# One scan of 1024 columns per state, with block 1's first value put in by a one-column product

## The chip, the cores and the metric

The kernel runs on one core of one Trainium2 chip. The metric is device time in microseconds from the start to the end of one launch. The five engines of the core each work through their own queue of instructions in program order and wait for one another by semaphores: TensorE (PE in the views, its weight loads PEld), VectorE (DVE), ScalarE (ACT), GpSimd (POOL) and SyncE (SP), which issues the DMAs.

## What is computed

Four layers follow one another on an input of 2 rows x 2048 tokens x 128 channels: a time-mix layer, a ternary feed-forward layer, a selective state-space layer and a mixture of experts. The change lies in the third:

```python
def _L1_attn_ref(x, W_in, conv_w, conv_b, W_x, W_dt, b_dt, A_log, D, W_out):
    ...                                   # raw, gate <- x @ W_in; h = silu(conv(raw) + conv_b)
    ts, Bmat, C = jnp.split(h @ W_x, [DTR, DTR + DST], axis=-1)
    dt = softplus(ts @ W_dt + b_dt)
    A = -exp(A_log)
    dA = exp(dt[..., None] * A)
    dBu = dt[..., None] * Bmat[:, :, None, :] * h[..., None]
    state = dA * state + dBu              # over the 2048 tokens, for 256 channels x 16 states
    y = sum over the states of state * C
    y = (y + h * D) * silu(gate)
    return y @ W_out
```

## The kernel before

The state-space layer (`phase_ssm`) keeps channels on partitions: 256 channels are two blocks (CB = 2) of 128 partitions, and tokens are the columns. The 2048 tokens of a row are cut in four pieces (t = 0 to 3) of N = 512 columns, and the pieces of the two rows (b = 0, 1) take turns, so that there are eight tiles (t, b). Within a tile the 16 states (n = 0 to 15) come one after the other. For each state:

- TensorE spreads row n of B over all partitions into a bank of PSUM with one bf16 product ("the spread product", line 1517, target `bcastB(n)`, which is the second block's half of `DD`; `DD` has two such pairs of banks, taken in turn, so that the product for state n waits until the scan of state n - 2 is done).
- ScalarE makes `dA` = exp(dt * -A), one instruction of 512 columns per block (line 1643).
- VectorE multiplies `dtu` (dt * h, both blocks) by the spread row, over both banks in one instruction of 1024 columns (line 1794, called dBu here), and then scans each block by itself: two instructions of 512 columns (line 1781), each starting from that block's column of `carry`.
- GpSimd multiplies the scanned states by the spread row of C (line 1734) and keeps the last column in `carry` (line 1727).
- TensorE adds the product to the sum over states with identity products in f32 (line 1503, three states later).

In between stand pieces of the next tile's preparation and of the last tile's end. On TensorE, after the spread product of state n: centring (n = 0, line 1421), variance (n = 1, 1426), the convolution in four parts (n = 2 to 5, line 1432), the gate's projection (n = 6, 1439), the skip product (n = 7), the x-projections (n = 8, 9, line 1446), dt (n = 10, 1453), and the last tile's output (n = 12 and 14). VectorE normalises the next tile after the scan of state 1 (line 1764, `xn`), for which the convolution waits, and scales the last tile's output after state 15 (line 1771). GpSimd adds and multiplies `dt` and `dtu` of the next tile at n = 12 and 13 (lines 1703, 1707). All of this order is written out by hand; no scheduler moves anything.

In the listings below, the scan and the product dBu of VectorE stand as one row each; a name like `pD` is the tile `DD`, `const` the identity, and `sel` the selectors of the spread product.

Of the kernel before, what the change touches and what calls it, by code (L numbers as in the profile page):

```python
# [5 lines left out]
F32 = mybir.dt.float32  # L6
# [28 lines left out]
for _name, _count in (  # L35
# [10 lines left out]
         "dt dtu bcastB c_out c_in0 c_in1 c_in2 c_in3 warm dA dBu scan kept prod acc y ygated skips "  # L46
# [1251 lines left out]
def phase_ssm(nc, G):  # L1298
# [9 lines left out]
    with mem:  # L1308
# [24 lines left out]
        carry = sb("carry3", [P, B, DST, CB])  # L1333
        raw = sb("raw3", [P, 2, 2 * FFN])
        YB = [mem.enter_context(nc.psum_tensor(f"pY3_{c}", [P, N], F32)) for c in range(CB)]

        DD = mem.enter_context(nc.psum_tensor("pD3", [P, 2 * CB, N], F32))
        c_rows = nc.dram_tensor("ssm_c", (NT * B, DST, N), F32, kind="Internal").ap()
# [20 lines left out]
        def dBu(n, c):  # L1359
            return DD[:, (n % 2) * CB + c, :]  # L1360

# [19 lines left out]
        def _(sp):  # L1381
# [8 lines left out]
            def rows_out(t, b):  # L1390
                sp.wait_ge(S["whole"], at(t, b))
                sp.dma_start(c_rows[t * B + b, :, :], rest[3 * BC - DST:3 * BC, b, :]).then_inc(S["c_out"], 16)

# [7 lines left out]
            rows_out(0, 0)  # L1401
            for t in range(NT):
                for b in range(B):
                    for n in range(DST):
# [7 lines left out]
                        if n == 12 and not (t == NT - 1 and b == B - 1):  # L1412
                            rows_out(*after(t, b))

        @block.tensor
        def _(pe):
# [94 lines left out]
            def body(t, b):  # L1511
                for n in range(DST):
# [4 lines left out]
                    nc.tensor.matmul(bcastB(n), G.sel[:, n, :], split[:, b, :], start=True, stop=True)\  # L1517
# [35 lines left out]
        def _(act):  # L1553
# [131 lines left out]
            act.wait_ge(S["carry0"], 3)  # L1685
# [5 lines left out]
        def _(pool):  # L1691
            def prep(t, b, step):
# [12 lines left out]
                elif step == 3:  # L1705
                    pool.wait_ge(S["dt"], at(t, b))
                    nc.gpsimd.tensor_tensor(dtu[:, b, :, :], dt[:, b, :, :], h[b][:, :, :], ALU.mult)\
                      .then_inc(S["dtu"], 1)

# [48 lines left out]
        def _(dve):  # L1758
# [15 lines left out]
            def scan(t, b, n):  # L1774
# [5 lines left out]
                for c in range(CB):  # L1780
                    last = nc.vector.tensor_tensor_scan(hs[:, slot(b, n), c, :], dA[:, slot(b, n), c, :],  # L1781
                                                        dBu(n, c), carry[:, b, n, c:c + 1],
                                                        ALU.mult, ALU.add)
                last.then_inc(S["scan"], 1)

            def body(t, b):
                for n in range(DST):
                    if n == 0:
                        dve.wait_ge(S["dtu"], at(t, b))
# [4 lines left out]
                    nc.vector.tensor_tensor(DD[:, (n % 2) * CB:(n % 2) * CB + CB, :], dtu[:, b, :, :],  # L1794
# [819 lines left out]
```

## Time and profile before

| what | us |
|---|---|
| median of 3 runs | 1310.34 |
| lowest and highest run | 1308.96, 1311.38 |
| span of the profiled execution | 1360.4 |
| scan stage in it, first dBu to last scan | about 485 |
| VectorE busy in the span | 986.3 (72%) |
| TensorE busy in the span | 1107.5 (81%) |

The profiled execution spans 1360.4 us, 50 us more than the median of the runs shown; durations below are from the profiled one. The views group instructions by line (with mean time of one), or list them in order of time, with the idle time of the engine before an instruction and the instruction that ended it. In the list of an engine, an instruction with a count (x4) is that many in a row, and its time is from the first start to the last end. PE's matmuls in f32 stand as two records each.

### The profile page before, as it was taken

To read this page: it belongs to the slowest core of one execution; us is meant where nothing else is said; L and a number is where in the kernel's file an instruction comes from. 1 tells how busy PE (TensorE), PEld (TensorE's weight loads), DVE (VectorE), ACT (ScalarE), POOL (GpSimd) and SP (SyncE) were. 2 spreads that over 40 slices of the span, in tenths; PEclk is the share of its full clock that TensorE was granted. 3 is DMA by queue.
4 is the path that set the end of the run, shared out by engine and by line. 5 is a ranking of instruction groups with operands and counts; after the bars stand their busy time and mean duration, and the time that the engine had idled before them with its cause. 6 is when DMAs were issued, how large, how long until landed. Compare 5 with 4: busy or idle time off the path is not lost. (4 is left out here: it accounts for less than half of the span.)

```text
span 1360.4 us, 16588 instructions
## 1 busy us (share of the span) xinstructions
PE 1107.5 (81%) x4914; PEld 554.2 (41%) x4914; DVE 986.3 (72%) x1333; ACT 730.8 (54%) x1163; POOL 733.0 (54%) x617
## 2 busy tenths in 40 slices
PE   6564779999999988797988989897883877877863
PEld 2221234444444423243333334332342665666653
DVE  6996775675755449999999999999928644544545
ACT  5765544555555366675766767575533333333444
POOL 0122342331413007898898898979831665656554
PEclk8775899999999988999999999998885989889886
DMA  6000000000000022332323222222101111111115
GB/s 218 0 1 0 0 1 1 0 1 0 0 0 1 0 63 80 90 98 68 107 64 102 88 83 70 76 72 68 57 8 54 37 42 38 42 39 44 36 37 185
DMA packets 32552, 67.07 MB, mean 49 GB/s; under 512 B 5760, under 2 KB 5952, under 8 KB 32256
## 3 DMA queue, kind: packets, MB, share of 16 engines
q1 hardware_dynamic: 27056, 55.16, 12.7%
q0 software_dynamic: 4992, 10.23, 2.9%
q8 instruction: 39, 0.64, 0.2%
q10 hardware_dynamic: 432, 0.76, 0.2%
q14 instruction: 33, 0.27, 0.1%
HBM read 56.57 MB, written 9.57 MB: 49 GB/s over the span
## 5 line engine op out<-in xcount | busy, mean ns | idle before, releaser
L1734 POOL TENSOR_TENSOR prod<-hs,csb 128x1024 f32<-128x1024 f32 x128 | 301.9, 2358 | 142.3 <-DVE hs L1781 141.6
L1781 DVE TENSOR_TENSOR_SCAN hs<-dA,carry,pD 128x512 f32<-128x512 f32 x256 | 313.8, 1267 | 5.6 <-DVE pD L1794 1.2
L1503 PE MATMUL pY<-prod,const 128*128 128x512 f32 x512 | 244.6, 601 | 1.8 <-POOL prod L1734 1.8
L1643 ACT ACTIVATE dA<-dt,negA 128x512 f32<-128x512 f32 x256 | 168.0, 713 | 17.2 <-POOL dt L1703 15.7
L1794 DVE TENSOR_TENSOR pD<-dtu,pD 128x1024 f32<-128x1024 f32 x128 | 155.7, 1216 | 9.2 <-PE pD L1517 9.1
L2507 DVE SCALAR_TENSOR_TENSOR hid<-pR,silu 128x512 f32<-128x512 f32 x78 | 53.8, 689 | 133.0 <-ACT silu L2215 114.6
L1503 PEld LDWEIGHTS pY<-prod,const 128*128 128x128 f32 x512 | 96.7, 192 | 117.7 <-issue 112.7
L2215 ACT ACTIVATE silu<-pR 128x512 f32<-128x512 f32 x78 | 46.5, 596 | 137.0 <-remote 77.2
L2280 POOL DMA_INDIRECT moe_outs<-y,to x78 | 84.0, 1077 | 66.3 <-ACT y L2207 45.6
L2261 POOL DMA_INDIRECT g<-moe_rows,source x78 | 79.6, 1020 | 68.5 <-issue 35.0
L1998 PE MATMUL pR<-x,moe_hi 128*128 128x256 f16 x312 | 92.3, 296 | 14.7 <-DVE x L2491 6.9
L987 ACT ACTIVATE stage<-pR,vec 128x512 f32<-128x512 f32 x64 | 43.9, 688 | 100.1 <-PE pR L687 99.9
L2000 PE MATMUL pR<-x,moe_lo 128*128 128x256 f16 x312 | 91.7, 294 | 5.5 <-issue 5.3
L1999 PE MATMUL pR<-x,moe_hi 128*128 128x256 f16 x312 | 91.8, 294 | 2.3 <-issue 1.9
L1432 PE MATMUL pQ<-xn,convw 128*128 128x512 f32 x112 | 61.6, 676 | 17.4 <-DVE xn L1764 17.4
L2110 PE MATMUL pY<-moe_hi,hid_hi 128*128 x312 | 64.1, 235 | 7.9 <-issue 7.2
L2111 PE MATMUL pY<-moe_lo,hid_hi 128*128 x312 | 63.7, 235 | 4.2 <-issue 4.2
L1037 POOL TENSOR_TENSOR z_lo<-z,z_hi 128x512 f16<-128x512 f32 x8 | 10.6, 1326 | 104.9 <-DVE z_hi L1124 104.9
L429 POOL TENSOR_TENSOR o<-o,rs 128x512 f32<-128x512 f32 x8 | 12.2, 1528 | 101.9 <-DVE o L549 101.9
L2112 PE MATMUL pY<-moe_hi,hid_lo 128*128 x312 | 63.8, 235 | 2.6 <-issue 2.6
L1517 PE MATMUL pD<-split,sel 96*128 96x512 bf16 x128 | 50.0, 391 | 19.0 <-DVE hs L1781 18.4
L1026 POOL TENSOR_TENSOR K_lo<-kstage,K_hi 128x512 f16<-128x512 f32 x24 | 28.8, 1205 | 53.7 <-DVE K_hi L1099 53.7
(422 smaller groups left out, 2591.0 us busy)
## 6 DMA issues: line engine op xcount, KB each, us to landing
csb<-ssm_c SPq DMA_DIRECT2D x128, 256.0 KB, 3.2
raw<-moe_w SPq DMA_DIRECT2D x12, 512.0 KB, 4.9
room<-moe_outs SPq DMA_DIRECT2D x8, 512.0 KB, 7.6
hidw<-hid_w SPq DMA_DIRECT2D x1, 2048.0 KB, 10.1
moe_rows<-xt SPq DMA_DIRECT2D x8, 256.0 KB, 2.0
outT<-X SPq DMA_DIRECT2D x8, 256.0 KB, 2.0
X<-xT SPq DMA_DIRECT2D x3, 512.0 KB, 4.2
g<-moe_rows,source POOLq DMA_INDIRECT x78
```

The costliest lines, as they stand in the source:

```text
L1503: last = nc.tensor.matmul(YB[c][:], G.ident, prod[:, slot(b, n), c, :], start=n == 0, stop=n == DST - 1)
L1643: last = nc.scalar.activation(dA[:, slot(b, n), c, :], dt[:, b, c, :], ACT.Exp, scale=negA[:, c, n:n + 1])
L1734: nc.gpsimd.tensor_tensor(prod[:, slot(b, n), :, :], hs[:, slot(b, n), :, :], csb[:, slot(b, n), :, :].to_broadcast([P, CB, N]), ALU.mult)\
L1781: last = nc.vector.tensor_tensor_scan(hs[:, slot(b, n), c, :], dA[:, slot(b, n), c, :], dBu(n, c), carry[:, b, n, c:c + 1], ALU.mult, ALU.add)
L1794: nc.vector.tensor_tensor(DD[:, (n % 2) * CB:(n % 2) * CB + CB, :], dtu[:, b, :, :], bcastB(n).unsqueeze(1).to_broadcast([P, CB, N]), ALU. ...
L1998: nc.tensor.matmul(out, w_hi, x_hi, start=start, stop=False)
L1999: nc.tensor.matmul(out, w_hi, x_lo, start=False, stop=False)
L2000: return nc.tensor.matmul(out, w_lo, x_hi, start=False, stop=stop)
L2110: nc.tensor.matmul(out, hid_hi[:, n % HR, at], w_hi, start=u == 0 and h == 0 and r == 0, stop=False)
L2112: last = nc.tensor.matmul(out, hid_lo[:, n % HR, at], w_hi, start=False, stop=u == 1 and h == 1 and r == 1)
L2261: nc.gpsimd.indirect_dma_start(g[:, i % GR, r, :], None, rows, bass.IndirectOffsetOnAxis(ap=source[:, 2 * i + r:2 * i + r + 1], axis=0))\
L2280: nc.gpsimd.indirect_dma_start(outs, bass.IndirectOffsetOnAxis(ap=to[:, 2 * i + r:2 * i + r + 1], axis=0), y[:, i % YR, r, :], None).then_ ...
```

## The change

The two scans of a state become one of 1024 columns that runs through both blocks. For this the first column is made to carry the start values. `dA`'s first column is fixed for good: 1 for block 0, 0 for block 1, so ScalarE's instructions now make 511 columns. `first` holds, per tile, block and state, the value of the first token: decay times carry plus fresh input. Block 0 gets it as the scan's initial value, with dBu's first column at 0 (column 0 of `dtu` is set to 0 for block 0). Block 1 gets it through dBu's first column: `dtu`'s first column is set to 1 there, and a new product of TensorE, the identity times one column of `first` in f32, overwrites column 0 of the spread row.

`first` is made once per tile: ScalarE computes the first token's decay (two instructions, 16 columns each), GpSimd does three small products and sums and two one-column fills after `dtu`, and SyncE sends the first column of B to memory and back, spread over the partitions (two more DMAs per tile). VectorE's wait for `dtu` at a tile's start becomes a wait for `first`, and TensorE waits for `first` at state 0 too. For the very first tile VectorE makes `first` itself.

```diff
+            def first_B(t, b):
+                sp.wait_ge(S["b_out"], 16 * at(t, b))
+                wait_past(sp, S["first"], at(t, b) - B)
+                sp.dma_start(B0[:, b, :], b_first[t * B + b:t * B + b + 1, :].to_broadcast([P, DST])).then_inc(S["b_in"], 16)
...
-                    nc.tensor.matmul(bcastB(n), G.sel[:, n, :], split[:, b, :], start=True, stop=True)\
+                    nc.tensor.matmul(bcastB(n), G.sel[:, n, :], split[:, b, :], start=True, stop=True)
+                    if n == 0:
+                        pe.wait_ge(S["first"], at(t, b))
+                    nc.tensor.matmul(bcastB(n)[:, 0:1], G.ident, first[:, b, CB - 1, n:n + 1], start=True, stop=True)\
                       .then_inc(S["bcastB"], 1)
...
-                    last = nc.scalar.activation(dA[:, slot(b, n), c, :], dt[:, b, c, :], ACT.Exp,
+                    last = nc.scalar.activation(dA[:, slot(b, n), c, 1:N], dt[:, b, c, 1:N], ACT.Exp,
...
+            def decay_first(t, b):
+                act.wait_ge(S["dt"], at(t, b))
+                wait_past(act, S["carried0"], at(t, b) - 2)
+                for c in range(CB):
+                    last = nc.scalar.activation(decay0[:, c, :], negA[:, c, :], ACT.Exp, scale=dt[:, b, c, 0:1])
+                last.then_inc(S["decay0"], 1)
...
+                    if not is_last(t, b) and n == 14:
+                        decay_first(*after(t, b))
...
+                    first_token(t, b)
+
+            def first_token(t, b):
+                pool.wait_ge(S["decay0"], at(t, b) - 1)
...
+                nc.gpsimd.tensor_tensor(first[:, b, :, :], decay0[:, :, :], carry[:, b, :, :].rearrange("p n c -> p c n"),
+                                        ALU.mult).then_inc(S["carried0"], 1)
+                pool.wait_ge(S["b_in"], 16 * at(t, b))
+                pool.wait_ge(S["dtu"], at(t, b))
+                nc.gpsimd.tensor_tensor(fresh0[:, :, :], dtu[:, b, :, 0:1].to_broadcast([P, CB, DST]),
+                                        B0[:, b, :].unsqueeze(1).to_broadcast([P, CB, DST]), ALU.mult).then_inc(S["fresh0"], 1)
+                pool.wait_ge(S["carried0"], at(t, b) - 1)
+                pool.wait_ge(S["fresh0"], at(t, b))
+                nc.gpsimd.tensor_tensor(first[:, b, :, :], first[:, b, :, :], fresh0[:, :, :], ALU.add)
+                nc.gpsimd.memset(dtu[:, b, 0, 0:1], 0.0)
+                nc.gpsimd.memset(dtu[:, b, 1, 0:1], 1.0).then_inc(S["first"], 1)
...
-                for c in range(CB):
-                    last = nc.vector.tensor_tensor_scan(hs[:, slot(b, n), c, :], dA[:, slot(b, n), c, :],
-                                                        dBu(n, c), carry[:, b, n, c:c + 1],
-                                                        ALU.mult, ALU.add)
-                last.then_inc(S["scan"], 1)
+                nc.vector.tensor_tensor_scan(hs[:, slot(b, n), :, :].rearrange("p c n -> p (c n)"),
+                                             dA[:, slot(b, n), :, :].rearrange("p c n -> p (c n)"),
+                                             both_dBu(n).rearrange("p c n -> p (c n)"), first[:, b, 0, n:n + 1],
+                                             ALU.mult, ALU.add).then_inc(S["scan"], 1)
...
-                        dve.wait_ge(S["dtu"], at(t, b))
+                        dve.wait_ge(S["first"], at(t, b))
```

In TensorE's order, state 6 of a tile of the middle loop stood like this before (the spread product, the gate's projection, the sum over states):

```order
L1517 MATMUL pD<-split,sel 128x512 [waits ssm_scan]
L1438 REGISTER_ALU
L1439 MATMUL pQ_0<-xn_1,ssmw 128x512 [waits ssm_parked]
L1438 REGISTER_ALU
L1439 MATMUL pQ_1<-xn_1,ssmw 128x512 [waits ssm_parked]
L1503 MATMUL pY_0<-prod,const 128x512 [waits ssm_prod]
L1503 MATMUL pY_1<-prod,const 128x512
```

and stands like this with the change:

```order
L1534 MATMUL pD<-split,sel 128x512 [waits ssm_scan]
L1537 MATMUL pD<-first,const 128x1
L1455 REGISTER_ALU
L1456 MATMUL pQ_0<-xn_1,ssmw 128x512 [waits ssm_parked]
L1455 REGISTER_ALU
L1456 MATMUL pQ_1<-xn_1,ssmw 128x512 [waits ssm_parked]
L1520 MATMUL pY_0<-prod,const 128x512 [waits ssm_prod]
L1520 MATMUL pY_1<-prod,const 128x512
```

One f32 product of one column has come in behind each spread product; nothing else moved. At a tile's start TensorE had, before, the spread product of state 0, the sum of the last tile's state 13, and the centring of the next tile:

```order
L1295 ISA [waits ssm_split3]
L1517 MATMUL pD<-split,sel 128x512 [waits ssm_scan]
L1499 ISA
L1503 MATMUL pY_0<-prod,const 128x512 [waits ssm_prod]
L1503 MATMUL pY_1<-prod,const 128x512
L1295 ISA
L1295 REGISTER_ALU [waits ssm_relu]
L1421 ISA [waits ssm_scaledC]
L1421 MATMUL pQ_0<-X,const 128x512
```

and has now:

```order
L1295 ISA [waits ssm_split3]
L1534 MATMUL pD<-split,sel 128x512 [waits ssm_scan]
L1537 MATMUL pD<-first,const 128x1 [waits ssm_first]
L1516 ISA
L1520 MATMUL pY_0<-prod,const 128x512 [waits ssm_prod]
L1520 MATMUL pY_1<-prod,const 128x512
L1295 ISA
L1295 REGISTER_ALU [waits ssm_relu]
L1438 ISA [waits ssm_scaledC]
L1438 MATMUL pQ_0<-X,const 128x512
```

The sum of state 13 and all that follows now stand behind the wait for `first`. On GpSimd, states 12 to 14 of a tile stood like this before (`dt`, then `dtu` of the next tile):

```order
L1703 TENSOR_TENSOR dt<-dt,dtu 128x1024 [waits ssm_log1p]
L1734 TENSOR_TENSOR prod<-hs,csb 128x1024 [waits ssm_acc,ssm_c_in1,ssm_scan]
L1727 COPY carry<-hs 128x2
L1707 TENSOR_TENSOR dtu<-dt,h 128x1024 [waits ssm_dt]
L1734 TENSOR_TENSOR prod<-hs,csb 128x1024 [waits ssm_acc,ssm_c_in2,ssm_scan]
```

and stand like this now:

```order
L1732 TENSOR_TENSOR dt<-dt,dtu 128x1024 [waits ssm_log1p]
L1782 TENSOR_TENSOR prod<-hs,csb 128x1024 [waits ssm_acc,ssm_c_in1,ssm_scan]
L1775 COPY carry<-hs 128x2
L1736 TENSOR_TENSOR dtu<-dt,h 128x1024 [waits ssm_dt]
L1746 TENSOR_TENSOR first<-decay_3,carry 128x32 [waits ssm_kept,ssm_decay0]
L1750 TENSOR_TENSOR fresh_3<-dtu,B_3 128x32 [waits ssm_dtu,ssm_b_in]
L1754 TENSOR_TENSOR first<-first,fresh_3 128x32 [waits ssm_fresh0,ssm_carried0]
L1755 MEMSET dtu 128x1
L1756 MEMSET dtu 128x1
L1782 TENSOR_TENSOR prod<-hs,csb 128x1024 [waits ssm_acc,ssm_c_in2,ssm_scan]
```

Five small instructions have come in between `dtu` and the product of state 14.

## Rows read from the trace of the kernel before

**Rows 1.** Groups by line, scan stage 505.5 to 995 us: count, busy us and mean ns, idle before.

```profile
L1781 DVE TENSOR_TENSOR_SCAN hs<-dA,carry,pD 128x512 f32<-128x512 f32 x256 | 313.8, 1267 | 5.6 <-DVE pD L1794 1.2
...
L1794 DVE TENSOR_TENSOR pD<-dtu,pD 128x1024 f32<-128x1024 f32 x128 | 155.7, 1216 | 9.2 <-PE pD L1517 9.1
...
L1727 POOL COPY carry<-hs 128x2 f32<-128x2 f32 x128 | 24.1, 188 | 0.0
```

**Rows 2.** VectorE in order of time, one tile: start us, us, engine, line [idle before].

```profile
763.58 1.23 DVE L1794 TENSOR_TENSOR pD<-dtu,pD 128x1024 f32<-128x1024 f32 x1 [0.41 <-PE pD L1517]
764.85 2.45 DVE L1781 TENSOR_TENSOR_SCAN hs<-dA,carry,pD 128x512 f32<-128x512 f32 x2
767.23 1.23 DVE L1794 TENSOR_TENSOR pD<-dtu,pD 128x1024 f32<-128x1024 f32 x1
...
789.88 1.23 DVE L1794 TENSOR_TENSOR pD<-dtu,pD 128x1024 f32<-128x1024 f32 x1 [0.33 <-PE pD L1517]
...
797.12 1.21 DVE L1794 TENSOR_TENSOR pD<-dtu,pD 128x1024 f32<-128x1024 f32 x1
```

**Rows 3.** TensorE in order of time, the same tile, states 2 to 5.

```profile
756.00 2.77 PE L1432 MATMUL pQ<-xn,convw 128*128 128x512 f32 x4 [2.48 <-DVE xn L1764]
...
763.16 0.38 PE L1517 MATMUL pD<-split,sel 96*128 96x512 bf16 x1
763.38 1.88 PE L1432 MATMUL pQ<-xn,convw 128*128 128x512 f32 x4
765.10 1.88 PE L1503 MATMUL pY<-prod,const 128*128 128x512 f32 x4
766.82 0.38 PE L1517 MATMUL pD<-split,sel 96*128 96x512 bf16 x1
```

**Rows 4.** TensorE's f32 products of 8 columns elsewhere: their weight loads; granted clock (PEclk) there.

```profile
1020.78 0.97 PEld L2018 LDWEIGHTS pX<-gatew,sgate 128*128 128x128 f32 x8
1020.80:1021.80 1.00, 1.00 (x12) 0.95 (x9) 0.32 (x1) 1.00 (x3) 0.92 (x1) 1.00 0.66 256
```

**Rows 5.** Groups by line and shape, whole span: shorter scans of VectorE.

```profile
L2379 DVE TENSOR_TENSOR_SCAN so_far<-keep,chosen 128x256 f16<-128x256 f16 x1 | 0.7, 691 | 0.0
L2392 DVE TENSOR_TENSOR_SCAN tiles_to<-one,tiles_of 128x8 f32<-128x8 f32 x1 | 0.2, 174 | 0.0
```

**Rows 6.** Order of time at a tile's start: GpSimd, VectorE and TensorE.

```profile
743.49 2.37 POOL L1707 TENSOR_TENSOR dtu<-dt,h 128x1024 f32<-128x1024 f32 x1
...
747.42 1.22 DVE L1794 TENSOR_TENSOR pD<-dtu,pD 128x1024 f32<-128x1024 f32 x1
...
743.37 0.39 PE L1517 MATMUL pD<-split,sel 96*128 96x512 bf16 x1 [1.50 <-DVE hs L1781]
...
747.67 1.12 PE L1421 MATMUL pQ<-X,const 128*128 x2 [2.19 <-DVE scaled L1771]
```

**Rows 7.** Busy time by stretch (PE, PEld, DVE, ACT, POOL), then granted clock: convolution of two tiles.

```profile
757.10:760.40 3.30, 3.30 (x6) 1.24 (x5) 3.29 (x3) 2.40 (x4) 1.38 (x3) 0.50 0.36 72
...
817.00:820.40 3.40, 3.40 (x9) 1.42 (x8) 3.37 (x4) 3.40 (x6) 1.50 (x3) 1.00 0.32 100
```

**Rows 8.** VectorE in order of time: the last step of a tile (three of seven).

```profile
624.79 0.67 DVE L1771 TENSOR_TENSOR scaled<-pQ,sq 128x512 f32<-128x512 f32 x1
...
807.96 0.66 DVE L1771 TENSOR_TENSOR scaled<-pQ,sq 128x512 f32<-128x512 f32 x1
...
927.83 0.67 DVE L1771 TENSOR_TENSOR scaled<-pQ,sq 128x512 f32<-128x512 f32 x1
```

**Rows 9.** One small instruction of GpSimd elsewhere: ns of it (shortest, median, longest).

```profile
L2250 POOL IOTA spare<- x1: 184/184/184, 1007.6 to 1007.6; 128x78 int32 x1
```

**Rows 10.** Start of the stage: the first DMA of C's rows, VectorE's dtu; landing times of eight.

```profile
499.59 0.33 SPq L1392 DMA_DIRECT2D ssm_c<-sq  x1
...
504.62 1.23 DVE L1836 TENSOR_TENSOR dtu<-dt,h 128x1024 f32<-128x1024 f32 x1
...
DMA to landing us min/median/max: 1.6/2.9/3.2
```

More of the change, by code:

```diff
@@ L45 @@
          "h xproj ts_in split1 whole rest1 split2 split3 dt_in magnitude expm log1p relu "
-         "dt dtu bcastB c_out c_in0 c_in1 c_in2 c_in3 warm dA dBu scan kept prod acc y ygated skips "
+         "dt dtu b_out b_in decay0 carried0 fresh0 first spliced bcastB c_out c_in0 c_in1 c_in2 c_in3 warm dA dBu scan kept prod acc y ygated skips "
          "down squaredC varianceC logC rstdC scaledC addedC w_in0 w_in1 w_high w_scaled w_low "
@@ L1333, in phase_ssm @@
         carry = sb("carry3", [P, B, DST, CB])
+        decay0 = sb("decay0_3", [P, CB, DST])
+        fresh0 = sb("fresh0_3", [P, CB, DST])
+        first = sb("first3", [P, B, CB, DST])
+        B0 = sb("B0_3", [P, B, DST])
         raw = sb("raw3", [P, 2, 2 * FFN])
@@ L1337, in phase_ssm @@
         DD = mem.enter_context(nc.psum_tensor("pD3", [P, 2 * CB, N], F32))
+        b_first = nc.dram_tensor("ssm_b", (NT * B, DST), F32, kind="Internal").ap()
         c_rows = nc.dram_tensor("ssm_c", (NT * B, DST, N), F32, kind="Internal").ap()
@@ L1401, in _ @@
             rows_out(0, 0)
+            first_B(0, 0)
             for t in range(NT):
@@ L1413, in _ @@
                             rows_out(*after(t, b))
+                        if n == 13 and not (t == NT - 1 and b == B - 1):
+                            first_B(*after(t, b))
         @block.tensor
@@ L1708, in prep @@
                       .then_inc(S["dtu"], 1)
+                    first_token(t, b)
+            def first_token(t, b):
+                pool.wait_ge(S["decay0"], at(t, b) - 1)
+                if is_start(t):
+                    pool.wait_ge(S["carry0"], 4)
+                else:
+                    pool.wait_ge(S["kept"], state(t, b, 0) - 1 - DST * (B - 1))
+                nc.gpsimd.tensor_tensor(first[:, b, :, :], decay0[:, :, :], carry[:, b, :, :].rearrange("p n c -> p c n"),
[9 more added lines that the diff above has]
+                nc.gpsimd.memset(dtu[:, b, 1, 0:1], 1.0).then_inc(S["first"], 1)
             def tail(t, b, step):
@@ L1793, in body @@
                     wait_past(dve, S["scan"], state(t, b, n) - 2)
-                    nc.vector.tensor_tensor(DD[:, (n % 2) * CB:(n % 2) * CB + CB, :], dtu[:, b, :, :],
+                    nc.vector.tensor_tensor(both_dBu(n), dtu[:, b, :, :],
                                             bcastB(n).unsqueeze(1).to_broadcast([P, CB, N]), ALU.mult)\
@@ L1836, in _ @@
             nc.vector.tensor_tensor(dtu[:, 0, :, :], dt[:, 0, :, :], h[0][:, :, :], ALU.mult).then_inc(S["dtu"], 1)
+            dve.wait_ge(S["b_in"], 16)
+            dve.wait_ge(S["dtu"], 1)
+            nc.vector.tensor_tensor(first[:, 0, :, :], dtu[:, 0, :, 0:1].to_broadcast([P, CB, DST]),
+                                    B0[:, 0, :].unsqueeze(1).to_broadcast([P, CB, DST]), ALU.mult).then_inc(S["fresh0"], 1)
+            dve.wait_ge(S["fresh0"], 1)
+            nc.vector.memset(dtu[:, 0, 0, 0:1], 0.0)
+            nc.vector.memset(dtu[:, 0, 1, 0:1], 1.0).then_inc(S["first"], 1)
             tiles(dve, body)
```

9 lines of the change are left out of this document (7 added, 2 removed).

## The prediction

> **What bounds the kernel now.** I read the groups by line of the scan stage first, then VectorE's and TensorE's instructions in order of time, then the granted clock by stretch. By the groups VectorE looks like the bound: 313.8 us of scans and 155.7 us of dBu, with 9.1 us lost to TensorE [rows 1], in a stage of about 485 us. The list in order of time says more. Left alone, VectorE needs 3.62 us per state (789.88 to 797.12 is two states) [rows 2]. From 763.58 to 789.88 it goes at TensorE's pace: at 763.58 it has stood 0.41 us for the spread product, and it starts the next dBu 3.65 us later [rows 2]. TensorE is full there: from one spread product to the next is 0.22 for itself, 1.72 for a part of the next tile's preparation and 1.72 for the sum over states, 3.66 us, with no gap [rows 3]. The seven states up to 789.88 took 26.30 us, 3.76 each, since the last two hold dearer products. So about half of a tile is TensorE's and the other half VectorE's; the two differ by hundredths of a microsecond per state, and the idle time charged to TensorE (9.1 us) is small only because both run nearly level.
>
> A tile has three legs, which I use for the sum. Leg A, from the convolution's start (756.00) to dBu of state 11 (789.88): 33.88 us, TensorE's. Leg B, from there to the next tile's first dBu: to 807.96 is 18.08, and 0.58 for the step that stands there makes 18.66, VectorE's. Leg C, from the first dBu (747.42) to the convolution: 8.58, VectorE's, since the convolution waits for xn. Together 61.12 [rows 2, 3, 6, 8]. Five tiles from 624.79 to 927.83 average 60.61 [rows 8].
>
> **What the change removes.** One scan instruction per state. A scan of 512 columns takes 1.267 us, the pair 2.45 from first start to last end [rows 1, 2]. One of 1024 adds 512 columns to the first: at 2.085 ns a column (between 8 and 256 columns) it takes 2.334 and saves 0.12; at 2.25 (between 256 and 512) 2.42, which saves 0.03 [rows 1, 5]. I take 0.12: the 256-column scan is f16, and the pitch of two f32 scans in a pair (2.45 - 1.27 = 1.18) leaves just 0.12 over 512 columns at 2.085. The ends stay for the range. If VectorE were the bound everywhere, 128 x 0.12 = 15 us would be the gain.
>
> "VectorE: DVE Perf Modes" of the Trainium skill, section on the TRN2 errata, has a fixed term of about 150 cycles per instruction, 156 ns; by it the same sum would be 20 us, while the pair's own pitch here leaves 0.12 us [rows 1, 2].
>
> **What it adds on TensorE.** A one-column f32 product per state, two records with a weight load each. No such product is in the trace; the nearest are the f32 products of 8 columns, whose 8 loads take 0.97 us at full clock, 0.12 per record, back to back [rows 4]. One load more can lie under the spread product, but the sum's first load, which lay there before, now comes out: two loads are added, 0.25 us per state. Lower end 0, if all lies under streaming products; upper end 0.37, three loads' worth, if none is covered. I take 0.25, the row nearest in kind.
>
> Leg A: at full clock it would be 32.1 before, for of its first 7.58 us (to 763.58) about 1.8 are the half clock seen from 757.10 to 760.40 (0.50, the 1.2 GHz level) [rows 2, 3, 7]. Nine new products (states 3 to 11) add 2.25: **34.35**. VectorE alone would now need 9 x 3.50, so TensorE holds it from state 6 or so.
>
> Leg B: five states at 0.12 less, 18.66 - 0.60 = 18.06, if `first` is there in time. `dtu` ends at 745.80, 1.62 before the first dBu (747.42) [rows 6]; with VectorE 0.36 faster over the three states in which GpSimd works on it, 1.26 are left. Between come three GpSimd instructions of 32 columns and two fills; small ones take 0.18 to 0.19 whatever they do [rows 1, 9], so five are 0.9 and the waits of one on the other 0 to 0.15 each: 0.9 to 1.3. Then the one-column product, 0.25 and its way to VectorE, 0.2 (the spread product needed 0.42 from start to dBu [rows 2, 3]). I take 1.5 in all and so a stall of 0.25 per tile (0.1 to 0.6): **18.31**.
>
> Leg C: VectorE's own is 8.58 - 2 x 0.12 = 8.34. But TensorE now stands still for `first`: it had been free from 741.87 and had done the sum of state 13 at 743.6; all that now starts at about 747 [rows 6]. From `first` on it must do the new product (0.25), the sum (1.72), the centring (0.86), spread and new product (0.47), sum (1.72), variance (0.86), again 0.47 and 1.72: 8.1 us, 7.6 after the first dBu. That fits in 8.34 at 2.4 GHz. But TensorE has then stood some 4.5 us with one spread product in it. Before, a wait of 2.48 us stood just ahead of the half clock at 757 [rows 3, 7], and the waits of 1.50 and 2.19 at the tile's start [rows 6] did not slow what followed. I expect the half clock at the tile's start instead of at the convolution, for about the 3.3 us it lasted before, of which 2.7 fall on work: 1.35 us lost, leg C **8.97**; and none at the convolution, since TensorE then reaches it about when xn does.
>
> Steady tile: 34.35 + 18.31 + 8.97 = 61.6 against 60.6: +1.0, six times +6. The first tile: +2.25 in leg A, -0.6 - 0.24 and +0.25 elsewhere, and at its start +0.8 (VectorE's own small steps and the product in front of the first dBu): +2.5. The new DMAs there are hidden: the first goes out with C's at 499.59, two landings of 1.6 to 3.2 end by 506.3 at the latest, about when dtu ends (505.85) [rows 10]. The last tile has fewer products beside the states, so VectorE's: at most -16 x 0.12 = -1.9, I take -1. Sum +7.5 us; the profiled span is 1360.4, 3.8% above the median, and scaling 7.5 by that changes nothing. **1310.3 + 7.5 = 1318.**
>
> **Costed at nothing.** ScalarE's 511 columns instead of 512; its two small decays, which wait for `dt` as its next instruction did anyway. Behind them now stands the output's last root; `dt` is ready before 743.49 and VectorE wants the root about 3.3 us later [rows 6, 8], room for four activations. SyncE's two DMAs per tile stand in a queue that runs four states ahead of GpSimd (`csb` has four slots); the second follows a weight transfer at n = 13 and has those four states to land. GpSimd's product of state 14 comes 1 us later; TensorE's sum of it comes later still.
>
> **Rivals.** (a) *The loads are hidden*, and VectorE's gain comes through. Leg A is then 32.1, B 18.2, C about 8.5: 58.8, 1.8 less per tile, with the first and last tiles -13 us: **1298**, faster. It decides at a product price under about 0.12. For it: loads run beside streaming products all through [rows 3, 7]. Against it: with 8 columns there is no stream to hide under, and the loads set the pace [rows 4]. "TensorE: Matmul & The Clock Gate" (step by step, the load phase) of the Trainium skill has loads pulled ahead of running matmuls, and (back-to-back issue gap) a floor of about 25 ns for so short a matmul; here a record took five times that [rows 4]. (b) *Half the price*, 0.12: 33.2 + 18.3 + 8.7 = 60.2, with the ends of the stage about **1308 to 1312**, no change. (c) *Two half-clock stretches per tile*, one at `first` and one at the convolution as before: 1.8 more per tile, **1328**. For it: the wait for xn is still there if VectorE is held longer than I think. (d) *The scan saves nothing* (1024 columns cost two of 512): legs B and C lose 0.84 per tile, **1324**.
>
> **How the numbers follow.** Forecast (1313 to 1322) 0.48; (a) 0.19; (b) 0.15, mostly within 0.2%; (c) 0.14; (d) 0.04. A measurement tells about 0.2%, 2.6 us, from no change. Faster 0.20, same 0.14, slower 0.66. The range 1302 to 1328 leaves out about half of (a) and the far end of (c).
>
> **What would show it.** In the changed trace: one scan of about 2.33 us per state; in states 6 to 11 dBu at a pitch of 3.90 us, with idle before it put down to the one-column product; TensorE without gaps there; at the tile's start a wait of over 4 us on TensorE for `first`, the clock at 0.50 behind it, and 1.00 at the convolution. A pitch of 3.66 in states 6 to 11 would show the price of the product wrong; a wait of VectorE for `first` of over 0.6 us, GpSimd's five instructions; a half clock at the convolution, the leg C.

## The result, and the profile after

The changed kernel is slower: 1338.8 us (median of four runs, 1336.1 to 1339.4) against 1309.7 for the kernel before in the same session, a ratio of 1.0201 with a 95% interval of 1.0178 to 1.0224. The forecast had the sign right and the size wrong: +7.5 us were expected and about +28 came (26 by the ratio, 29 by the medians), 11 us above the upper end of the range.

The groups of the whole run, from the page of the changed kernel (line, engine, operation, count; busy us, mean ns; idle time before it and what ended it):

```profile
L1828 DVE TENSOR_TENSOR_SCAN hs<-dA,first,pD 128x1024 f32<-128x1024 f32 x128 | 300.4, 2347 | 5.2 <-DVE pD L1841 0.8
L1841 DVE TENSOR_TENSOR pD<-dtu,pD 128x1024 f32<-128x1024 f32 x128 | 156.0, 1218 | 32.3 <-PE pD L1537 31.8
...
L1537 PE MATMUL pD<-first,const 128*128 128x1 f32 x256 | 37.9, 217 | 23.5 <-POOL dtu L1756 22.1
```

Against [rows 1]: the scans went from 313.8 to 300.4 us busy, one of 2.347 us in place of a pair, as the change means. VectorE's wait for TensorE ahead of dBu rose from 9.1 to 31.8 us. The scan did its part, then, and TensorE took it back with more. A group that was too small for the first page is as telling, VectorE's copy of three columns (the convolution's overlap with the last tile): count, shortest, median and longest ns, first and last start, of the kernel after and of the kernel before:

```profile
L1810 DVE COPY xn<-xn x6: 2006/2007/2243, 579.4 to 903.3; 128x3 f32<-128x3 f32 x6
```

```profile
L1762 DVE COPY xn<-xn x6: 141/144/145, 573.4 to 874.9; 128x3 f32<-128x3 f32 x6
```

The same instruction on the same 128x3 elements, untouched by the diff, takes fourteen times as long.

**Where in the tile.** VectorE of the changed kernel in order of time: dBu of the states 6, 9 and 11 (680.85), the tile's end (698.40), and on to the next normalized input:

```profile
660.98 1.23 DVE L1841 TENSOR_TENSOR pD<-dtu,pD 128x1024 f32<-128x1024 f32 x1
...
672.58 1.23 DVE L1841 TENSOR_TENSOR pD<-dtu,pD 128x1024 f32<-128x1024 f32 x1 [0.24 <-PE pD L1537]
...
680.85 1.23 DVE L1841 TENSOR_TENSOR pD<-dtu,pD 128x1024 f32<-128x1024 f32 x1 [0.55 <-PE pD L1537]
...
698.40 0.67 DVE L1819 TENSOR_TENSOR scaled<-pQ,sq 128x512 f32<-128x512 f32 x1
699.30 1.23 DVE L1841 TENSOR_TENSOR pD<-dtu,pD 128x1024 f32<-128x1024 f32 x1 [0.23 <-PE pD L1537]
700.56 2.35 DVE L1828 TENSOR_TENSOR_SCAN hs<-dA,first,pD 128x1024 f32<-128x1024 f32 x1
...
704.78 1.23 DVE L1841 TENSOR_TENSOR pD<-dtu,pD 128x1024 f32<-128x1024 f32 x1 [1.87 <-PE pD L1537]
706.04 2.35 DVE L1828 TENSOR_TENSOR_SCAN hs<-dA,first,pD 128x1024 f32<-128x1024 f32 x1
708.84 2.01 DVE L1810 COPY xn<-xn 128x3 f32<-128x3 f32 x1 [0.45 <-ACT sq L1578]
710.88 0.69 DVE L1812 TENSOR_TENSOR xn<-pQ,sq 128x512 f32<-128x512 f32 x1
```

GpSimd's product beside that copy ends at 710.83, the copy at 710.85:

```profile
708.47 2.36 POOL L1782 TENSOR_TENSOR prod<-hs,csb 128x1024 f32<-128x1024 f32 x1 [1.04 <-DVE hs L1828]
```

And TensorE of the same stretch:

```profile
695.04 0.39 PE L1534 MATMUL pD<-split,sel 96*128 96x512 bf16 x1 [1.06 <-DVE hs L1828]
698.67 0.58 PE L1537 MATMUL pD<-first,const 128*128 128x1 f32 x2 [3.25 <-POOL dtu L1756]
699.12 3.76 PE L1520 MATMUL pY<-prod,const 128*128 128x512 f32 x4
702.67 1.73 PE L1438 MATMUL pQ<-X,const 128*128 x2
704.24 0.38 PE L1534 MATMUL pD<-split,sel 96*128 96x512 bf16 x1
...
711.63 0.70 PE L1449 MATMUL pQ<-xn,convw 128*128 128x512 f32 x1 [2.04 <-DVE xn L1812]
```

Its granted clock (the third number from the end; before it busy us of PE, PEld, DVE, ACT, POOL) at that start, and at a convolution in the middle of the stage:

```profile
696.80:698.50 1.70, 0.00 (x0) 0.00 (x0) 1.70 (x2) 0.42 (x1) 1.56 (x5) 0.64 0.30 100
698.50:700.20 1.70, 1.52 (x4) 1.01 (x5) 1.47 (x2) 0.00 (x0) 1.46 (x4) 0.50 0.02 5
700.20:701.90 1.70, 1.70 (x4) 0.67 (x3) 1.66 (x2) 0.00 (x0) 1.70 (x3) 0.50 0.00 0
701.90:703.60 1.70, 1.70 (x4) 0.67 (x3) 1.01 (x1) 0.00 (x0) 1.70 (x2) 0.50 0.41 142
703.60:705.30 1.70, 1.70 (x7) 0.87 (x6) 0.52 (x1) 0.86 (x2) 1.70 (x4) 0.86 0.24 83
646.90:650.30 3.40, 3.31 (x10) 1.75 (x11) 3.36 (x3) 3.40 (x6) 0.00 (x0) 1.00 0.22 77
```

TensorE stands 3.25 us for `first`, and what follows runs at the 1.2 GHz level: the sum over states takes 3.76 us where [rows 3] have 1.88, the centring 1.73. Counted over the slices the half clock lasts 6.8 us, here and at the start of each of the other five tiles of the middle; before, it stood at the convolution [rows 7], for 3.4 us, in four of them. At the convolution the clock is now whole.

By the three legs of the forecast, a tile of the middle against its forecast (the convolution of this tile starts at 646.99, that of the next at 711.63):

| leg | before | forecast | after |
|---|---|---|---|
| A, convolution to dBu of state 11 | 33.88 | 34.35 | 680.85 - 646.99 = 33.86 |
| B, to the next tile's first dBu | 18.66 | 18.31 | 699.30 - 680.85 = 18.45 |
| C, to the convolution | 8.58 | 8.97 | 711.63 - 699.30 = 12.33 |

Tile ends of the changed kernel lie at 633.61 and 957.48 with four between, 64.77 us a tile against 60.61 [rows 8]; six such tiles make 25 of the 26 to 29 us. Legs A and B are within 0.5 us of the forecast. **All that was not foreseen lies in leg C**, 3.4 us per tile. VectorE's list has it: 1.87 stood for state 1's row (its spread and column product), 0.45 for the root, and 1.87 more in the copy, 4.2 together. The rest of the 12.33 is 8.1 of VectorE's own work, where the forecast had 8.34.

### The profile page after: what moved, and what is told of

It is laid out like the page before. It is cut to its first block and busy times, and to the rows that moved or that the text cites. A ratio compares the mean times of both kernels' runs of the same rounds, so it can differ in the third digit from the quotient of the medians.

```text
span 1336.7 us, 17080 instructions
## 1 busy us (share of the span) xinstructions
PE 1102.6 (82%) x5170; PEld 576.5 (43%) x5170; DVE 992.3 (74%) x1210; ACT 736.6 (55%) x1177; POOL 738.4 (55%) x652
## 5 line engine op out<-in xcount | busy, mean ns | idle before, releaser
L1828 DVE TENSOR_TENSOR_SCAN hs<-dA,first,pD 128x1024 f32<-128x1024 f32 x128 | 300.4, 2347 | 5.2 <-DVE pD L1841 0.8
L1520 PE MATMUL pY<-prod,const 128*128 128x512 f32 x512 | 259.7, 632 | 0.9 <-POOL prod L1782 0.9
L1841 DVE TENSOR_TENSOR pD<-dtu,pD 128x1024 f32<-128x1024 f32 x128 | 156.0, 1218 | 32.3 <-PE pD L1537 31.8
L1663 ACT ACTIVATE dA<-dt,negA 128x511 f32<-128x511 f32 x256 | 167.6, 712 | 1.5 <-DVE dt L1883 1.4
L2317 POOL DMA_INDIRECT g<-moe_rows,source x78 | 82.5, 1058 | 55.7 <-issue 46.8
L2054 PE MATMUL pR<-x,moe_hi 128*128 128x256 f16 x312 | 86.2, 276 | 1.2 <-DVE x L2547 1.2
L2055 PE MATMUL pR<-x,moe_hi 128*128 128x256 f16 x312 | 86.3, 277 | 0.0
L2056 PE MATMUL pR<-x,moe_lo 128*128 128x256 f16 x312 | 86.1, 276 | 0.0
L1537 PEld LDWEIGHTS pD<-first,const 128*128 128x128 f32 x256 | 49.8, 198 | 67.9 <-issue 38.3
L1449 PE MATMUL pQ<-xn,convw 128*128 128x512 f32 x112 | 56.9, 631 | 16.3 <-DVE xn L1812 16.3
L1534 PE MATMUL pD<-split,sel 96*128 96x512 bf16 x128 | 48.9, 382 | 11.3 <-DVE hs L1828 11.3
L2166 PE MATMUL pY<-moe_hi,hid_hi 128*128 x312 | 56.9, 220 | 0.8 <-DVE hid_lo L2554 0.8
L1537 PE MATMUL pD<-first,const 128*128 128x1 f32 x256 | 37.9, 217 | 23.5 <-POOL dtu L1756 22.1
```

The source lines that it names most:

```text
L1449: last = nc.tensor.matmul(Q[c][:], convw[:, c, k, :], xn[b][:, k:k + N], start=k == 0, stop=k == TAPS - 1)
L1520: last = nc.tensor.matmul(YB[c][:], G.ident, prod[:, slot(b, n), c, :], start=n == 0, stop=n == DST - 1)
L1537: nc.tensor.matmul(bcastB(n)[:, 0:1], G.ident, first[:, b, CB - 1, n:n + 1], start=True, stop=True)\
L1663: last = nc.scalar.activation(dA[:, slot(b, n), c, 1:N], dt[:, b, c, 1:N], ACT.Exp, scale=negA[:, c, n:n + 1])
L1828: nc.vector.tensor_tensor_scan(hs[:, slot(b, n), :, :].rearrange("p c n -> p (c n)"), dA[:, slot(b, n), :, :].rearrange("p c n -> p (c n)" ...
L1841: nc.vector.tensor_tensor(both_dBu(n), dtu[:, b, :, :], bcastB(n).unsqueeze(1).to_broadcast([P, CB, N]), ALU.mult)\
```

## The experiments

Ratios are to the kernel before, run beside it; a difference between two changed kernels is given by these ratios and by the medians, which disagree by 1 to 2 us. The theory had two parts: the half clock behind TensorE's wait for `first`, and a copy on VectorE that has to wait for something on GpSimd. The rival was that the one-column product costs more than thought all along the tile.

**The copy first.** In the changed kernel, VectorE's copy is moved ahead of its wait for the root:

```diff
-                dve.wait_ge(S["rstd"], at(t, b))
                 if not is_start(t):
                     nc.vector.tensor_copy(xn[b][:, 0:TAPS - 1], xn[b][:, N:N + TAPS - 1]).then_inc(S["halo"], 1)
                     dve.wait_ge(S["halo"], at(t, b) - B)
+                dve.wait_ge(S["rstd"], at(t, b))
```

> The changed kernel with one edit: VectorE's copy of three columns ahead of xn is issued before the wait for the normalising root instead of behind it. Theory: in the changed kernel the copy lasts 2.0 to 2.2 us (0.14 before) because the root is 0.3 to 0.45 us late, so that GpSimd's product of state 1 has begun and the copy ends only with it; ahead of the wait the copy comes directly behind the scan, before GpSimd starts. Then it lasts 0.14 again and six tiles get back about 2.0 us each: 1339 - 12 = 1327. Rival: the copy is long for a reason that does not hang on what GpSimd runs then; it stays at 2 us and the time at 1339.

Measured 1327.4, ratio 1.0125 (1.0095 to 1.0155): 10 us below the changed kernel by the ratios, 11.4 by the medians. The copy is short again:

```profile
L1809 DVE COPY xn<-xn x6: 142/144/145, 578.7 to 886.6; 128x3 f32<-128x3 f32 x6
```

So the copy's length hangs on its place. The half clock with its late spread product is still there, but shorter; VectorE's dBu of state 1 in one tile, then TensorE's clock there:

```profile
698.38 1.23 DVE L1841 TENSOR_TENSOR pD<-dtu,pD 128x1024 f32<-128x1024 f32 x1 [1.10 <-PE pD L1537]
```

```profile
693.60:697.00 3.40, 3.40 (x6) 1.32 (x6) 3.35 (x3) 0.00 (x0) 3.40 (x3) 0.50 0.03 11
697.50:699.00 1.50, 1.50 (x7) 0.81 (x6) 0.61 (x1) 0.95 (x2) 1.50 (x3) 1.00 0.31 90
```

In five of the six tiles of the middle the clock is low for 3.4 us instead of 6.8, behind the same wait (3.24 us in this tile), and dBu of state 1 waits 0.73 to 1.10 us in place of 1.63 to 1.94. A tile takes 61.58 us instead of 64.77: 1.9 of this is the copy itself, and most of the rest is this shorter wait. Why the low stretch shrank is open. In the two traces the scan stage is 17.9 us shorter and the stage behind it 5.0 us longer, so that the 10 to 11 us of the whole kernel are not the price of the copy alone.

**The copy late in the kernel before.** The inverse: the kernel before, with a fill of 512 columns between the wait and the copy, so that the copy comes when GpSimd has begun its next product.

```diff
                 if not is_start(t):
+                    nc.vector.memset(pause[:, :], 0.0)
                     nc.vector.tensor_copy(xn[b][:, 0:TAPS - 1], xn[b][:, N:N + TAPS - 1]).then_inc(S["halo"], 1)
```

> The kernel before with one small fill of 512 columns (0.49 us) on VectorE between the scan of state 1 and the copy of three columns, in six tiles. Theory: the fill lets GpSimd's product of state 1 start first, and the copy, which lasted 0.14 us, then ends only with that product: 0.5 + 1.7 to 2.0 us per tile, about 6 x 2.3 = 14 us above the kernel before, copy at about 1.9 us. Rival: the copy stays at 0.14 us and the fill costs its own 3 us.

Measured 1331.5, ratio 1.0152 (1.0127 to 1.0177), +20 us. In order of time, all engines, one tile:

```profile
703.07 0.48 DVE L1763 MEMSET pause<- 128x512 f32 x1
703.09 2.35 POOL L1735 TENSOR_TENSOR prod<-hs,csb 128x1024 f32<-128x1024 f32 x1 [0.41 <-DVE hs L1783]
...
703.47 2.00 DVE L1764 COPY xn<-xn 128x3 f32<-128x3 f32 x1
```

GpSimd's product ends at 705.44 and the copy at 705.47. A fill of 0.48 us beside the same product is not held up; the copy is held until the product is over. The mechanism is shown with nothing of the change in the kernel. The excess over the +14 expected goes with more half clock in the middle of the stage, from the first copy on: 37.5 us in seven stretches where the kernel before has 13.7 in four; that this is its whole cause is argued, not tested.

**TensorE's order.** In the changed kernel, the wait for `first` and the column product of state 0 go behind the sum of state 13 and the centring:

```diff
-                    if n == 0:
-                        pe.wait_ge(S["first"], at(t, b))
-                    nc.tensor.matmul(bcastB(n)[:, 0:1], G.ident, first[:, b, CB - 1, n:n + 1], start=True, stop=True)\
-                      .then_inc(S["bcastB"], 1)
+                    if n > 0:
+                        put_first(t, b, n)
...
+                    if n == 0:
+                        pe.wait_ge(S["first"], at(t, b))
+                        put_first(t, b, 0)
```

> The changed kernel with TensorE's order at a tile's start altered: the wait for first and the one-column product of state 0 stand behind the sum of state 13 and the next tile's centring instead of ahead of them. Theory: TensorE's wait for first and the half clock behind it make the spread product of state 1 late (1.6 to 2.0 us of VectorE's wait per tile), then the root (0.3 to 0.45), then the copy (2.0): all three go, about 4 us per tile, 1339 - 6 x 4 = 1315. The price of the product itself (0.22 per state) stays. Rival: the product's price is the main loss and the wait is not; then under 8 us are gained.

Measured 1317.5, ratio 1.0052 (1.0035 to 1.0069), as expected: 20 (by the ratios) to 21 us hang on that one wait's place. (The trace is of a run of 1330 us; two of its six copies are long there.)

**Both edits together.**

> The changed kernel with both edits: TensorE's wait for first behind the sum of state 13 and the centring, and VectorE's copy ahead of the wait for the root. Theory: in the altered order alone the copy still met GpSimd's product in two of six tiles of the profiled execution (1.9 us each); that goes too: 1317 - 4 = 1313, the copy 0.14 us in all six. Rival: the wait only moves to xn, which wants the root anyway: 1317 again.

Measured 1321.1, ratio 1.0071 (1.0054 to 1.0087): a miss, no better than the order alone. Its copies are all 0.14 us in the trace (of a run of 1316.8 us), so in its ordinary runs the order alone probably keeps them short already; this is not shown. Part of what is left is in VectorE's list:

```profile
689.50 0.67 DVE L1824 TENSOR_TENSOR scaled<-pQ,sq 128x512 f32<-128x512 f32 x1
691.59 1.23 DVE L1846 TENSOR_TENSOR pD<-dtu,pD 128x1024 f32<-128x1024 f32 x1 [1.42 <-PE pD L1529]
```

The first dBu of a tile now waits 1.42 us for the column product, which stands behind a centring that itself waits for `scaled`. The order trades one wait for another. And the clock still falls for 3.4 us behind the start of four tiles: the sum that starts at 692.37 takes 3.49 us.

**Idle products in the wait.** In the changed kernel, 14 bf16 products with an unused result fill TensorE's wait for `first`:

```diff
                     if n == 0:
+                        if not is_first(t, b):
+                            for _ in range(14):
+                                nc.tensor.matmul(dBu(n, 0), G.sel[:, 0, :], G.sel[:, 0:4, :].rearrange("p n m -> p (n m)"),
+                                                 start=True, stop=True)
                         pe.wait_ge(S["first"], at(t, b))
```

> The changed kernel, with 14 idle bf16 products on TensorE (into a bank that is free then, read by nobody) between the spread product of state 0 and the wait for first, some 3 us of work in the wait; the order and all waits stay. Theory: the half clock that follows the wait (0.51 over 5 us) is what makes the spread product of state 1 and the root late; at full clock the work behind first takes 2.6 us less, the root is there in time, the copy is 0.14 us again: 3 to 4 us per tile, 1339 - 20 = 1319. Rival: work that starts only with first is late at either clock: the clock gives 1.5 us per tile, the root stays late and the copy long: about 1330.

Measured 1315.9, ratio 1.0029 (1.0009 to 1.0049), 22 to 23 below the changed kernel. What is left of TensorE's wait for `first`, the granted clock of the stretch behind it, then VectorE's list:

```profile
690.90 0.38 PE L1541 MATMUL pD<-first,const 128*128 128x1 f32 x2 [0.21 <-POOL dtu L1760]
```

```profile
691.40:696.50 5.10, 5.10 (x15) 2.34 (x15) 5.03 (x4) 1.81 (x3) 5.10 (x5) 1.00 0.19 53
```

```profile
691.32 1.23 DVE L1845 TENSOR_TENSOR pD<-dtu,pD 128x1024 f32<-128x1024 f32 x1
...
694.85 1.21 DVE L1845 TENSOR_TENSOR pD<-dtu,pD 128x1024 f32<-128x1024 f32 x1
...
698.40 1.17 DVE L1814 COPY xn<-xn 128x3 f32<-128x3 f32 x1
```

The wait itself is still there, on the same semaphore in the same place, with idle products in all but its last 0.21 us; work behind it starts no earlier, but the clock is whole. It falls in none of the six tiles of the middle. The 1.87 us that VectorE stood for the spread product of state 1 are gone. So the loss at the tile's start is the half clock and what follows from it, not the wait. The copy still meets GpSimd's product (0.70 us on average).

**The product alone.** The kernel before, with a column product of zeros added to each spread product:

```diff
-                    nc.tensor.matmul(bcastB(n), G.sel[:, n, :], split[:, b, :], start=True, stop=True)\
+                    nc.tensor.matmul(bcastB(n), G.sel[:, n, :], split[:, b, :], start=True, stop=False)
+                    nc.tensor.matmul(bcastB(n)[:, 0:1], G.ident, nought[:, 0:1], start=False, stop=True)\
                       .then_inc(S["bcastB"], 1)
```

> The kernel before with the one-column f32 product alone behind each spread product (it adds a column of zeros, so nothing of the result changes), two scans as before, no new wait. Theory: TensorE's states in the middle of a tile go from 3.65 to 3.87 us, nine of them per tile, so about 2 us in seven tiles: 1311 + 14 = 1325. Rival: the weight loads are hidden and the time stays within 4 us of the kernel before.

Measured 1328.1, ratio 1.0131 (1.0106 to 1.0156), +15 by the medians, +17 by the ratio: the product is not hidden. Two of the six copies are long in its trace (2.30 us each), 4.3 us that are not the product's own. TensorE's list, a state of the middle:

```profile
704.68 0.28 PE L1519 MATMUL pD<-nought,const 128*128 128x1 f32 x2
704.82 1.96 PE L1433 MATMUL pQ<-xn,convw 128*128 128x512 f32 x4
706.62 1.88 PE L1504 MATMUL pY<-prod,const 128*128 128x512 f32 x4
708.34 0.38 PE L1518 MATMUL pD<-split,sel 96*128 96x512 bf16 x1
708.56 0.28 PE L1519 MATMUL pD<-nought,const 128*128 128x1 f32 x2
```

One state is 3.88 us (704.68 to 708.56) where [rows 3] have 3.66 (763.16 to 766.82): 0.22 more, the product and its two loads.

**The scan alone.** The kernel before with the merged scan, block 1 running on from block 0:

```diff
-                for c in range(CB):
-                    last = nc.vector.tensor_tensor_scan(hs[:, slot(b, n), c, :], dA[:, slot(b, n), c, :],
-                                                        dBu(n, c), carry[:, b, n, c:c + 1], ALU.mult, ALU.add)
-                last.then_inc(S["scan"], 1)
+                nc.vector.tensor_tensor_scan(hs[:, slot(b, n), :, :].rearrange("p c n -> p (c n)"),
+                                             dA[:, slot(b, n), :, :].rearrange("p c n -> p (c n)"),
+                                             DD[:, (n % 2) * CB:(n % 2) * CB + CB, :].rearrange("p c n -> p (c n)"),
+                                             carry[:, b, n, 0:1], ALU.mult, ALU.add).then_inc(S["scan"], 1)
```

> The kernel before with the one scan of 1024 columns alone (left out is block 1's own start value: its states run on from block 0's last column). Theory: the scan saves 0.12 us per state, but only in the seven states that VectorE holds, 0.8 us per tile, and in the last tile 1.9: 1311 - 8 = 1303. Rival: VectorE is the bound throughout: 128 x 0.12 = 15 us, 1296.

Measured 1305.0, ratio 0.9946 (0.9930 to 0.9963): the scan's whole gain is 7 to 8 us, somewhat over half of 128 times what one state saves (0.10 us). That TensorE's pace takes the rest was expected and is not shown. The trace, of a run of 1300.4 us, has the wait of dBu for TensorE at 11.3 us, only 2.2 more than before, and a scan stage 10.7 us shorter, with half clock in one tile of the middle instead of four:

```profile
L1793 DVE TENSOR_TENSOR pD<-dtu,pD 128x1024 f32<-128x1024 f32 x128 | 155.3, 1213 | 12.2 <-PE pD L1517 11.3
```

**The change without its product.** The changed kernel without the column product and TensorE's wait, alone and then with the copy first:

```diff
-                    if n == 0:
-                        pe.wait_ge(S["first"], at(t, b))
-                    nc.tensor.matmul(bcastB(n)[:, 0:1], G.ident, first[:, b, CB - 1, n:n + 1], start=True, stop=True)\
                       .then_inc(S["bcastB"], 1)
```

> The changed kernel without the one-column product and without TensorE's wait for first (VectorE still waits for first; left out is block 1's start value, so that its states start from zero). Theory: against the kernel with the altered order it shows the product alone: states 6 to 11 fall back from 3.88 to 3.65 us, about 1.6 to 2 us per tile in seven tiles, so 12 us below it, about 1303. Rival: TensorE's price is hidden and it comes out within 4 us of the altered order.

> The same two edits, without the one-column product and TensorE's wait for first (left out is block 1's start value). Theory: against the kernel with both edits it is the product's price alone, 0.22 us in the states that TensorE holds, about 1.3 to 2 us per tile: 9 to 12 us below it, about 1303. Rival: under 4 us below it: the product is hidden once the order is right.

Measured 1313.0, ratio 1.0011 (0.9989 to 1.0032), and 1310.0, ratio 0.9975 (0.9951 to 0.9999). The first was a miss by 10 us. Part of the reason is the copy, here with VectorE's wait for the root ahead of it:

```profile
L1807 DVE COPY xn<-xn 128x3 f32<-128x3 f32 x6 | 4.9, 814 | 2.4 <-ACT sq L1575 2.3
```

The six copies take 4.9 us together, 4 more than before. But this trace is of a run of 1304.4 us, 9 below the median, so the rest of the miss stays open. With the copy first it still takes 0.82 us on average: the scan of state 1 now ends while GpSimd is in its product of state 0, so the copy is too early there, as it is too late in the changed kernel. The second lies 11 us below the run of both edits (1321.1), which has the product, its loads and VectorE's 1.42 us for it at each tile's start: the product's price once more, and the wait for it.

**Idle products in the kernel before.** Eight in one place (behind the sum of state 15), then six behind the sum of state 13 and six behind that of state 15:

```diff
-                    nc.tensor.matmul(bcastB(n), G.sel[:, n, :], split[:, b, :], start=True, stop=True)\
-                      .then_inc(S["bcastB"], 1)
+                    spread = nc.tensor.matmul(bcastB(n), G.sel[:, n, :], split[:, b, :], start=True, stop=True)
+                    fill = {0: 6, 2: 6}.get(n, 0) if not is_first(t, b) and not is_last(t, b) else 0
+                    if not fill:
+                        spread.then_inc(S["bcastB"], 1)
                     if n < LAG and not is_first(t, b):
                         accumulate(*before(t, b), DST - LAG + n)
+                    if fill:
+                        for _ in range(fill):
+                            last = nc.tensor.matmul(dBu(n, 0), G.sel[:, 0, :], G.sel[:, 0:4, :].rearrange("p n m -> p (n m)"),
+                                                    start=True, stop=True)
+                        last.then_inc(S["bcastB"], 1)
```

> The kernel before with 8 idle bf16 products on TensorE behind the sum of state 15, in the 2.5 us in which it waits for xn ahead of the convolution. Theory: the half clock at the convolution, seen in four of six tiles and worth 1.5 to 2 us each, goes: 1311 - 7 = 1304, tiles of 59.2 us throughout. Rival: the clock falls all the same, or VectorE takes the time: no change.

> The kernel before with idle bf16 products on TensorE in two of its waits: 6 behind the sum of state 13 (a wait of about 2.2 us for the last tile's scaled output) and 6 behind the sum of state 15 (the wait for xn). With 8 in the second place alone the clock still fell in four tiles. Theory: with both waits filled TensorE keeps its clock through the tile's start, tiles of 59.2 us, 1312 - 7 = 1305, faster than either kernel. Rival: the fills end before the waits do and the clock falls again, or VectorE waits for the fills what the clock gives: within 3 us of the kernel before.

Eight in one place: 1311.3, ratio 0.9999 (0.9980 to 1.0018), a miss. The clock still fell in four tiles (the last of them is without idle products), now within 2.3 us of the tile's end instead of at the convolution, and dBu stood 3.8 us in all for the idle products. Six and six: 1305.5, ratio 0.9955 (0.9938 to 0.9973), faster than both kernels. With these two fills the clock falls in none of the six tiles of the middle. Its clock from a tile's end through the next convolution, and its dBu:

```profile
684.50:696.50 12.00, 10.41 (x28) 4.50 (x29) 11.86 (x13) 9.02 (x15) 10.06 (x9) 1.00 0.25 76
```

```profile
L1801 DVE TENSOR_TENSOR pD<-dtu,pD 128x1024 f32<-128x1024 f32 x128 | 155.0, 1211 | 4.5 <-PE pD L1517 4.4
```

The wait of dBu for TensorE halves from 9.1 to 4.4, for 6 us of the whole.

**The kernel before once more**, for its long first span.

> The kernel before once more, for a second profile: the first one's span was 50 us longer than its timed runs. Theory: the scan stage is as in the first profile (first dBu to the last output step about 485 us) and the excess lay in the stage behind it; here the span is about 1308 and the stage behind about 305 us. Rival: the profile stretches the scan stage too, and durations read from it were too long by 3 to 4%.

Measured 1312.4 with a span of 1312.8. Its scan stage lasts 484.4 us, from the first dBu (510.59) to the last step (995.02), as in the first profile (505.88 to 990.57, 484.7): the first profile's extra time lay behind this stage, and its rows may be read as they stand.

## Why the prediction was right in sign and wrong in size

**Right: the two prices and their net.** The merged scan was put at 2.334 us and is 2.347; the product at 0.25 per state and is 0.22; the pitch of states 6 to 11 at 3.90 and is 3.87 up to state 9, and 3.97 on the mean of all five (660.98 to 680.85), since the last two hold dearer products. Scan alone -7 to -8, product alone +15 to +17: together some +7 to +10, where the forecast had +7.5. That the totals lie so close is in part luck, since the 7.5 also hold a stall for `first` and a half clock moved from one place to another, and the run of the product alone holds two long copies. Rival (a), the loads hidden, falls with the product alone. Rivals (b), half the price, and (d), a scan that saves nothing, fall with the same two runs.

**Right: leg B.** GpSimd's five small instructions end at 698.62, 0.88 us after `dtu` (697.74); VectorE stood 0.23 us for `first` and its product, where 0.25 was taken. Of the five, the three on 32 columns took 0.25 to 0.26 each and the fills 0.10, where 0.18 to 0.19 was taken for any. The last tile gave 62.74 - 62.07 = 0.7 back, where 1 was taken.

**Right in effect: leg A.** 33.86 against 34.35. The clock was whole at the convolution, as expected, so the product's nine times 0.22 took just the place of the 1.8 us that the half clock had cost there.

**Wrong: leg C, the step "for about the 3.3 us it lasted before, of which 2.7 fall on work: 1.35 us lost".** The half clock was put in the right place, with the wait that brings it, and its length was copied from another place. It lasted 6.8 us. All work from `first` (698.67) to the spread product of state 1 (704.24) fell into it: 5.57 us, where the forecast's own pieces, 0.25, 1.72 and 0.86, make 2.83. That is 2.7 us lost, twice the term. The trace of the kernel before held a stretch as long, in its last tile, which the forecast left aside (busy us of the five engines, then the clock):

```profile
944.80:951.60 6.80, 5.33 (x7) 2.05 (x8) 5.34 (x5) 4.84 (x8) 6.80 (x7) 0.50 0.14 49
```

The slack of leg C took some, and 1.87 us came through as VectorE's wait. Rival (c), two half-clock stretches, had the same fault: its second stretch was priced at 1.8, and the one that came cost, with the copy it made late, more than both.

**Missing: the copy.** Leg C took "VectorE's own" 8.34 with the copy at its old 0.14 us, and "Costed at nothing" spoke of another root, that of the last tile's output. The normalising root, for which the copy waits, was taken to be in time; that holds only while the spread product of state 1 is. It came 1.87 us late, the variance after it, and the root 0.45 late for VectorE. In the kernel before, the copy ended just ahead of GpSimd's next product, as a stretch of its trace shows:

```profile
755.07 0.14 DVE L1762 COPY xn<-xn 128x3 f32<-128x3 f32 x1
...
755.32 2.36 POOL L1734 TENSOR_TENSOR prod<-hs,csb 128x1024 f32<-128x1024 f32 x1 [0.92 <-DVE hs L1781]
```

A gap of 0.11 us was all its room. A root 0.45 us late lets GpSimd go first, and the copy pays the rest of a product of 2.36 us. Both rows stood in the trace beforehand, and both instructions hang on the same scan's end. With the copy first, leg C of the changed kernel is 9.53 us (693.67 to 703.20), 0.56 above its forecast: the copy, with the longer half clock that went with it, is most of the 3.4 us missed. "SBUF — State Buffer" of the Trainium skill, section "Who interferes with whom", has the rule: copies can use both of VectorE's port pairs, one of which GpSimd shares, and whichever of the two instructions comes second waits for the other's end. The trace agrees: the copies end 0.02 and 0.03 us after the product (710.85 against 710.83 in the changed kernel, 705.47 against 705.44 in the run with the late copy), while the scans, with GpSimd busy through most of them, stay at 2345 to 2349 ns.

**The sum, then:** +7 to +10 from scan and product, +20 to +23 from the tile's start (taken away by the other order, or by idle products), of which 11.6 lie inside the six copies (12.5 us against 0.9). That makes 27 to 33, and 26 to 29 were measured (by the ratio, or by the medians); the run of the product alone holds two long copies of its own, so the two terms overlap by some 4 us. What is still open: how the excess of the late-copy run divides, and why the half clock lasts 3.4 us in one place and 6.8 in another, even behind the same wait.

## What to carry to other kernels

A wait put ahead of work that does not need it can slow the work behind it too: price the work behind it at half clock for as long as the longest low stretch that the trace shows, not the nearest one. Where two engines are nearly level, look for the small instructions that slip in just ahead of something (here a copy 0.11 us ahead of GpSimd's product) and ask what they cost if they come late. An operation that saves 0.1 us on one engine and adds 0.2 on the other gains nothing in a stage that both share by halves; a gain was in the clock, which twelve idle products per tile bought without touching the scan.

## What the runs showed of the hardware

- A 128x3 f32 copy on VectorE takes 0.14 us alone and up to 2.3 us when a GpSimd product is running: it ends with that product. A fill of 512 columns in the same place took its ordinary 0.48 us.
- Low-clock stretches at TensorE lasted 3.4 us at the convolutions of the kernel before, and 6.8 us in the changed kernel behind a wait of 3.25 us that followed another of 1.06 us, with one bf16 product between. With only VectorE's copy moved, waits of 3.24 and 1.06 us in the same places were followed by 3.4 us, so the waits alone do not set the length.
- Idle bf16 products kept the clock whole through that wait (14 of them, -22 to -23 us); in the kernel before, eight in one of two waits did not, six in each of two did (-6 us).
- A one-column f32 product between two 512-column products added 0.22 us to TensorE's time per state, as two records with a load each.
